# RWKV attention and a small mixture of experts on one core: weights in column blocks, the first input chunk on a second DMA queue, and the first key mixes built another way

## What is computed

```python
shifted = jnp.pad(hidden, ((0, 0), (1, 0), (0, 0)))[:, :-1]
key   = hidden * time_mix_key   + shifted * (1.0 - time_mix_key)
value = hidden * time_mix_value + shifted * (1.0 - time_mix_value)
rec   = hidden * time_mix_receptance + shifted * (1.0 - time_mix_receptance)
k, v, r = key @ Wk, value @ Wv, jax.nn.sigmoid(rec @ Wr)
rwkv = _wkv(time_decay, time_first, k, v)   # a scan over the tokens
x = _layernorm(x + (r * rwkv) @ Wo)
# then: router over 8 experts, top 2, silu, gated sum, residual, layer norm
```

## Time and profile before

| | us |
|---|---|
| median of three runs | 459.97 (459.67 to 460.25) |
| profiled execution, first to last instruction (span) | 458.2 |
| TensorE busy | 444.6 (97% of the span) |
| VectorE busy | 404.1 (88%) |
| ScalarE busy | 356.0 (78%) |
| GpSimd busy | 312.0 (68%) |

### The profile page before, as it was taken

One profiled execution on the slowest core, in us unless ns is written; L12 is line 12 of the kernel. 1 busy time (PEld: TensorE's weight loads), 2 busy tenths in 40 slices (PEclk: granted clock), 3 DMA queues, 4 the chain that ended last, 5 costly groups with the idle time before them and its releaser, 6 DMA issues.

```text
span 458.2 us, 6679 instructions
## 1 busy us (share of the span) xinstructions
PE 444.6 (97%) x1984; PEld 340.2 (74%) x1984; DVE 404.1 (88%) x616; ACT 356.0 (78%) x801; POOL 312.0 (68%) x300
## 2 busy tenths in 40 slices
PE   8999999999999999999999999999999999999993
PEld 3444567777888888888888888888888888888761
DVE  5989989899788989999898998989898996876976
ACT  1666757877888779888788888888798887768695
POOL 2355677588658998579858797569966694744334
PEclk9999999999999999999999999999999999999998
DMA  8703230033000042002320042100520022300016
GB/s 239 223 0 117 93 92 1 1 115 93 1 1 0 2 160 92 24 0 74 135 70 0 1 139 93 46 0 24 162 93 1 1 69 94 137 1 0 0 49 229
DMA packets 20244, 30.64 MB, mean 67 GB/s; under 512 B 2032, under 2 KB 7152, under 8 KB 20208
## 3 DMA queue, kind: packets, MB, share of 16 engines
q1 hardware_dynamic: 20208, 30.21, 20.3%
HBM read 21.82 MB, written 8.39 MB: 66 GB/s over the span
## 4 chain that ended last, share of the span: by engine, by line
PE 78%; DVE 5%; ACT 2%; POOL 2%; issue 1%; ACTq 0%; DVEq 0%
PE PH L449 5%; PE PV L330 5%; PE PV L336 5%; PE PV L331 5%; PE PR L336 5%; PE PR L330 5%; PE PK L330 5%; PE PR L331 5%; PE PK L336 5%; PE PK L331 5%; PE PP L359 4%; PE PP L360 4%; PE PP L364 4%; PE PT L431 3%; PE PP L379 2%
## 5 line engine op out<-in xcount | busy, mean ns | idle before, releaser
L592 ACT ACTIVATE PR<-PR 128x512 f32<-128x512 f32 x128 | 74.6, 583 | 29.8 <-PE PR L336 10.6
L1213 POOL TENSOR_TENSOR DQ<-DEN,EX 128x512 f32<-128x512 f32 x32 | 41.3, 1290 | 20.6 <-DVE DEN L871 20.6
L1219 POOL TENSOR_SCALAR NM<-SUM,RS 128x1 f32<-128x1 f32 x30 | 8.0, 267 | 62.1 <-ACT RS L592 62.1
L330 PE MATMUL PK<-KH,WKH 128*128 128x512 f32 x112 | 46.2, 413 | 0.6 <-DVE NUM L888 0.6
L925 DVE SCALAR_TENSOR_TENSOR KT<-D,VEC,XT 128x512 f32<-128x512 f32 x57 | 45.8, 851 | 0.0
L330 PE MATMUL PV<-VH,WVH 128*128 128x512 f32 x112 | 45.6, 407 | 0.0
L336 PE MATMUL PR<-RL,WRH 128*128 128x512 f32 x112 | 44.0, 393 | 0.7 <-POOL RL L1181 0.7
L330 PE MATMUL PR<-RH,WRH 128*128 128x512 f32 x112 | 44.5, 398 | 0.2 <-DVE RW L912 0.2
L336 PE MATMUL PV<-VL,WVH 128*128 128x512 f32 x112 | 43.9, 392 | 0.0
L336 PE MATMUL PK<-KL,WKH 128*128 128x512 f32 x112 | 43.9, 392 | 0.0
L331 PE MATMUL PK<-KH,WKL 128*128 128x512 f32 x112 | 43.8, 391 | 0.0
(11 more groups left out here) (275 smaller groups left out, 1285.7 us busy)
## 6 DMA issues: line engine op xcount, KB each, us to landing
XT<-in_xt SPq DMA_DIRECT2D x32, 256.0 KB, 3.3
XN<-in_x SPq DMA_DIRECT2D x28, 256.0 KB, 2.7
out<-XN SPq DMA_DIRECT2D x28, 256.0 KB, 2.0
X1T<-in_wo SPq DMA_DIRECT2D x1, 1024.0 KB, 5.1
XT<-in_x SPq DMA_DIRECT2D x4, 256.0 KB, 4.2
out<-XT SPq DMA_DIRECT2D x4, 256.0 KB, 2.4
X1T<-in_wk SPq DMA_DIRECT2D x2, 256.0 KB, 4.9
XN<-in_wv SPq DMA_DIRECT2D x2, 256.0 KB, 5.7
```

The source lines that it names most:

```text
L330: eng.matmul(dst[:, :], wh[:, c, o], high[:, c, :], start=(c == 0), stop=False)
L592: eng.activation(*a, **k).then_inc(q[s], 1)
L1213: eng.tensor_tensor(DQ[:, :], DEN[:, 0:T], EX[:, 1, :], ALU.add).then_inc(q["e"], 1)
```

## The change

Three things are changed together. (1) The host lays the three weight matrices out as `[partition, column block, 4 x 128]`, so that one column block is 2 KB without a gap in each partition; loads, products and low parts index them accordingly. `key(4)` now waits only for the first half of the low parts of wk. (2) Input chunk 0 is requested by ScalarE's queue before its table load; SP requests VEC, the first block of wk and then input chunks 1, 2, 3; the remaining blocks follow in another order (wk 1, wv 0, wr 0, wk 2-3, wv 1, wr 1, wv 2-3, wr 2-3). (3) The four key mixes of batch 0 no longer use D: ScalarE makes y = (1 - mix) * shifted into the mix's own tile, with OMK = 1 - mix computed by VectorE from VEC, and VectorE makes hidden * mix + y in place (`first_mix`). GpSimd makes all four differences of batch 0, and VectorE's `difference` goes. Beside these, the dummy products fall from four to two.

```diff
-            def load_w(dst, src, s, lo=0, hi=H):
-                eng.dma_start(dst[:, :, lo:hi], src.rearrange("(c p) n -> p c n", p=128)[:, :, lo:hi])\
-                   .then_inc(q[s], 16)
+            def load_blocks(which, i):
+                dst, src = ((X1T, wk), (XN[0], wv), (XN[1], wr))[which]
+                lo, hi = ((0, 1), (1, 2), (2, C))[i]
+                eng.dma_start(dst[:, lo:hi, :], src[:, lo:hi, :]).then_inc(q[f"ws{which}{i}"], 16)
 
             eng.dma_start(VEC[:, :, :], vec).then_inc(q["vec"], 16)
-            load_xt(0, 0)
+            load_blocks(0, 0)
             load_xt(0, 1)
-            load_w(X1T, wk, "ws00", 0, 128)
             load_xt(0, 2)
             load_xt(0, 3)
-            for i, (lo, hi) in enumerate(((0, 128), (128, 256), (256, H))):
-                if i:
-                    load_w(X1T, wk, f"ws0{i}", lo, hi)
-                load_w(XN[0], wv, f"ws1{i}", lo, hi)
-                load_w(XN[1], wr, f"ws2{i}", lo, hi)
+            for which, i in ((0, 1), (1, 0), (2, 0), (0, 2), (1, 1), (2, 1), (1, 2), (2, 2)):
+                load_blocks(which, i)
@@ tensor
-                    last = eng.matmul(dst[:, :], stage[:, c, o], full(0, which, c), start=(c == 0), stop=(c == C - 1))
+                    last = eng.matmul(dst[:, :], stage[:, u, 128 * c:128 * c + 128], full(0, which, c), start=(c == 0), stop=(c == C - 1))
...
-                    eng.wait_ge(q[("lwk", "lwv", "lwr")[which]], j + 1 if which else 2)
+                    eng.wait_ge(q[("lwk", "lwv", "lwr")[which]], j + 1 if which else j // 2 + 1)
...
-            for _ in range(4):
+            for _ in range(2):
                 eng.matmul(PP[:, :], RW[:, 0, 0:128], RW[:, 0, :], start=True, stop=True)
@@ scalar
+            eng.dma_start(XT[:, 0, 1:T + 1], xt[0, 0:128, :]).then_inc(q["xt0"], 16)
             eng.preload_act_table_set(TABLES)
...
             act("etd", NTD, VEC[:, 0, :], ACT.Exp)
+            eng.wait_ge(q["om"], 1)
+            eng.wait_ge(q["cm"], 1)
+            for c in range(C):
+                eng.wait_ge(q[f"xt{c}"], 16)
+                act("y", full(0, 0, c), XT[:, c, 0:T], ACT.Copy, scale=OMK[:, c:c + 1])
@@ vector
+            def first_mix(c):
+                eng.wait_ge(q[f"xt{c}"], 16)
+                eng.wait_ge(q["y"], c + 1)
+                eng.scalar_tensor_tensor(out=full(0, 0, c), in0=XT[:, c, 1:T + 1], scalar=VEC[:, 2, c:c + 1],
+                                         in1=full(0, 0, c), op0=ALU.mult, op1=ALU.add).then_inc(q["kt"], 1)
...
+            eng.wait_ge(q["vec"], 16)
+            eng.tensor_scalar(OMK, VEC[:, 2, :], -1.0, 1.0, ALU.mult, ALU.add).then_inc(q["om"], 1)
...
-            difference(1)
-            mixes(0, 0, 0, 1)
-            difference(3)
-            mixes(0, 0, 2, 3)
+            for c in range(C):
+                first_mix(c)
             mixes(0, 1, 0, 1)
@@ gpsimd
-            difference(0, 0)
-            difference(0, 2)
+            for c in range(C):
+                difference(0, c)
...
-                    o = slice(128 * j, 128 * j + 128)
-                    eng.tensor_tensor(low[:, :, o], stage[:, :, o], high[:, :, o].bitcast(F32), ALU.subtract)\
+                    eng.tensor_tensor(low[:, j, :], stage[:, j, :], high[:, j, :].bitcast(F32), ALU.subtract)\
@@ host
+    def blocks(w):
+        return np.ascontiguousarray(np.asarray(w).reshape(C, 128, C, 128).transpose(1, 2, 0, 3)).reshape(128, C, H)
```

More of the change, by code:

```diff
@@ L49, in rwkv_moe_postln @@
         VEC = sb("VEC", [128, 5, C])
-        CST = sb("CST", [128, 4, C])
+        CST = sb("CST", [128, 5, C])
         XT = sb("XT", [128, C, T + 1])
@@ L86, in rwkv_moe_postln @@
         UPT = KT[:, 1, :]
-        TD, NTD, CC, QB = (CST[:, i, :] for i in range(4))
+        TD, NTD, CC, QB, OMK = (CST[:, i, :] for i in range(5))
         def full(b, which, c):
@@ L251, in store, with load_rows @@
                 eng.dma_start(out[b, 128 * n:128 * n + 128, :], xn_at(NT * b + n)).then_inc(q[f"out{n}"], 16)
[L253 to L255 removed]
+            def load_rows(dst, src, s, n=H):
+                eng.dma_start(dst[:, :, 0:n], src.rearrange("(c p) n -> p c n", p=128)).then_inc(q[s], 16)
+            def load_blocks(which, i):
+                dst, src = ((X1T, wk), (XN[0], wv), (XN[1], wr))[which]
+                lo, hi = ((0, 1), (1, 2), (2, C))[i]
+                eng.dma_start(dst[:, lo:hi, :], src[:, lo:hi, :]).then_inc(q[f"ws{which}{i}"], 16)
             eng.dma_start(VEC[:, :, :], vec).then_inc(q["vec"], 16)
[L258 removed]
+            load_blocks(0, 0)
             load_xt(0, 1)
[L260 removed]
             load_xt(0, 2)
             load_xt(0, 3)
[L263 to L267 removed]
+            for which, i in ((0, 1), (1, 0), (2, 0), (0, 2), (1, 1), (2, 1), (1, 2), (2, 2)):
+                load_blocks(which, i)
             for c in range(C):
@@ L272, in _ @@
             eng.wait_ge(q["k"], C)
-            load_w(X1T, wo, "wo")
-            load_w(DR, dr, "dr", 0, HD)
+            load_rows(X1T, wo, "wo")
+            load_rows(DR, dr, "dr", HD)
             eng.wait_ge(q["lwv"], C)
@@ L310, in whole @@
             def whole(dst, stage, u, which):
-                o = slice(128 * u, 128 * u + 128)
                 eng.wait_ge(q[f"ws{which}{min(u, 2)}"], 16)
@@ L325, in split @@
                     eng.wait_ge(q["hw"], which + 1)
-                    eng.wait_ge(q[("lwk", "lwv", "lwr")[which]], j + 1 if which else 2)
+                    eng.wait_ge(q[("lwk", "lwv", "lwr")[which]], j + 1 if which else j // 2 + 1)
                 for c in range(C):
+                    o = slice(128 * c, 128 * c + 128)
                     if first:
                         eng.wait_ge(q["hi"], C * (3 * (b - 1) + which) + c + 1)
-                    eng.matmul(dst[:, :], wh[:, c, o], high[:, c, :], start=(c == 0), stop=False)
-                    eng.matmul(dst[:, :], wl[:, c, o], high[:, c, :], start=False, stop=False)
+                    eng.matmul(dst[:, :], wh[:, j, o], high[:, c, :], start=(c == 0), stop=False)
+                    eng.matmul(dst[:, :], wl[:, j, o], high[:, c, :], start=False, stop=False)
                     if first and C * (3 * (b - 1) + which) + c + 1 == ODD:
@@ L335, in split @@
                         eng.wait_ge(q["lo"], by_pool(C * (3 * (b - 1) + which) + c + 1))
-                    last = eng.matmul(dst[:, :], wh[:, c, o], low[:, c, :], start=False, stop=(c == C - 1))
+                    last = eng.matmul(dst[:, :], wh[:, j, o], low[:, c, :], start=False, stop=(c == C - 1))
                     if j == C - 1 and c < C - 1:
@@ L914, in mix @@
             def mix(b, which, c):
-                if b:
-                    eng.wait_ge(q["d"], C // 2 + C * (b - 1) + c + 1)
-                else:
-                    eng.wait_ge(q["d0" if c % 2 else "d"], c // 2 + 1)
+                eng.wait_ge(q["d"], C * b + c + 1)
                 if b and which < 2:
@@ L1038, in _ @@
             eng.tensor_scalar(QB, CC, -1.0, CLIP, ALU.mult, ALU.add).then_inc(q["cc"], 1)
-            def difference(c):
-                eng.wait_ge(q[f"xt{c}"], 16)
-                if c == 1:
-                    eng.wait_ge(q["cm"], 1)
-                eng.tensor_tensor(D[:, c, :], XT[:, c, 1:T + 1], XT[:, c, 0:T], ALU.subtract).then_inc(q["d0"], 1)
             def low_weights(lo):
@@ L1338 @@
         "vec": np.ascontiguousarray(np.stack(rows).transpose(2, 0, 1)),
-        "wk": np.ascontiguousarray(L0_attn_Wk),
-        "wv": np.ascontiguousarray(L0_attn_Wv),
-        "wr": np.ascontiguousarray(L0_attn_Wr),
+        "wk": blocks(L0_attn_Wk),
+        "wv": blocks(L0_attn_Wv),
+        "wr": blocks(L0_attn_Wr),
         "wo": np.ascontiguousarray(L0_attn_Wo),
```

1 line of the change is left out of this document (removed), and 2 rows, old and new, of the table q.

## The result

| | median us | ratio to before |
|---|---|---|
| before, beside it | 460.11 (459.67 to 460.95, 4 runs) | |
| after | 463.92 (463.82 to 464.44, 4 runs) | 1.0083 (95%: 1.007 to 1.0095) |

A forecast was written before the change was run, and what follows sets the result against it. The prediction took TensorE's pace to bound the kernel once started, so its time follows the start of `scan_max(0)`. Gains of 0.8 us (landing) and 0.7 us (shorter chain), all else nothing, gave 458.5 us, range 457.5 to 459.7.

The forecast's parts named there:

- So whatever moves the start earlier moves the whole: Start of the kernel: a shift there moves the whole 450 us behind it; the rest matters only if it slows the steady part.
- Layout and the wait of `key(4)`: nothing: Weight loads, low parts and the start of `key(4)`: claimed to cost or gain nothing.
- Chunk 3 lands at 7.0: Last input chunk at the start: lands at 7.0 and not 7.8, gain 0.8 us, bounds 0.4 and 1.7.
- rival B: Start: chunk 3 comes no sooner (7.8) or part is given back; only 0.7 us gained, 459.3 us; chance 0.18.
- From landing to `scan_max(0)`, 2.76 us: Start, chunk 3's landing to `scan_max(0)`: y, mix 3 and two value mixes take 2.76 us, 0.67 us gained.
- GpSimd's differences beside the mixes: Start: four GpSimd differences beside VectorE's mixes cost 0 to 0.42 us for each of three mixes; taken as 0.
- rival C: TensorE at the start: clock doesn't rise at about 5 us, `scan_max(0)` 0.65 us later, 460.6 or 463.6 us; chance 0.09.
- The second queue: Chunk 0 requested by ScalarE: the first issue comes 0.44 us sooner; by the skill's rule alone chunk 3 lands at 7.37.
- The signs of being wrong: Profile after: 0.85 us spacing in `key(0)`, y 3 starting after 7.5, or `value(1)`'s gain absent at 100 us.
- The sum: Whole kernel: span 458.2 less 1.5 gives 456.7 us; with 1.8 us around it, 458.5 us.

The follow-up runs named there:

- b_blocks: The kernel before with only the weights in column blocks, old request order on SP's one queue: 460.90 us, ratio 1.0015.
- b_cst5: The kernel before with only CST enlarged from four rows to five, the fifth unused: 462.76 us, ratio 1.0055.
- a_bm: The changed kernel with each weight column block as a separate contiguous 256 KB in memory: 463.21 us, ratio 1.0065.
- a12_xt1first: The changed kernel with CST of twelve rows, and SP requesting chunk 1 ahead of wk block 0: 462.82 us, ratio 1.0059.
- best1: The changed kernel with CST of 20 rows, padding before TH, chunk 1 before wk block 0, four dummies, GpSimd's differences 2 and 3 after six mixes: 459.24 us.
- a12_gate: The changed kernel with CST of twelve rows, and GpSimd making differences 1 to 3 only after the four key mixes: 463.83 us, ratio 1.0083.
- a12_oneq: The changed kernel with CST of twelve rows, and chunk 0 requested by SP, no DMA on ScalarE: 464.41 us, ratio 1.0093.

## Why the prediction was wrong, step by step

**"So whatever moves the start earlier moves the whole."** Right, with the other sign: 1.27 us at `scan_max(0)`, 1.26 at `value(1)` (23.15 for 21.89) and 1.23 at 100 us. The other half of that sentence, that the rest matters only if it slows the steady part, was right too, and was not followed up.

**"Layout and the wait of `key(4)`: nothing."** This is the step that failed most. The layout does cost nothing (b_blocks, spacing 229.6). But the change has another edit, one more row in CST, which the prediction only weighed as work for VectorE. It moved every tile behind it by 32 bytes and cost about 2.5 to 2.75 us (b_cst5 2.55). No term of the sum, no rival and no bound covered it. The one thing in the trace of before that hinted at it is that projections were spaced 234.2 ns and the others 229.6 although all are the same operation.

**"Chunk 3 lands at 7.0", bounds 6.07 and 7.37.** It landed at 8.07, outside the bounds and later than before. The first piece came 0.15 later than the model has it (3.41 for 0.72 + 1.6 + 0.94 = 3.26). The model, a constant time for each piece, failed: from chunk 0 to chunk 1 lie 3.3 us for two pieces, and then only 0.67 us for each. The later pieces are faster than any bound I took (0.75), the gap ahead of them was in no row I read. Its cause stays open. With contiguous blocks chunk 3 landed at 7.57 (a_bm), and with chunk 1 in second place at 7.26 (a12_xt1first), inside the bounds, but with the same requests at 7.97 in best1. The starting point was one trace too: four other traces with the loads of before have chunk 3 at 7.3 to 7.8, so that a step of 0.8 was hardly more than the spread of the thing it was measured from. The prediction put rival B's landing at 7.8 as the worst case.

**From landing to `scan_max(0)`, 2.76 us.** It took 4.50. ScalarE's y took 0.72 instead of 0.62 (0.10). Mix 3 could start at 8.86 then and started at 9.80 (0.94), because mix 2 still held VectorE: it had waited behind a difference and took 1.52. That the chunks came only 0.67 us apart is not the reason: in a12_gate they came as close, and mix 3 started 0.83 after its y did, as 8.95 would be here. So 0.09 of the 0.94 is the step from y to mix and 0.85 is GpSimd. Mix 3 held VectorE for 1.44 us and not 0.66 (0.78, GpSimd again). The value mixes were 0.08 shorter. 0.10 + 0.94 + 0.78 - 0.08 = 1.74, which is the difference; 1.63 of it is the turns that VectorE and GpSimd take.

**GpSimd's differences beside the mixes, "I take 0", bound 0.42 each.** This term of the sum was mis-sized, by reading the early rows from one side only. The mix beside the difference at 6.74 was this one of the kernel before:

```profile
6.29 0.74 DVE L925 SCALAR_TENSOR_TENSOR DR<-D,VEC,XT 128x512 f32<-128x512 f32 x1
```

It started first, ended at 7.03 and kept its 0.74; the difference started second, ended at 7.93, 0.90 after it, and paid with 1.19 for 1.03. Near 57 us the mix started second: GpSimd's instruction ends at 58.28 and the mix at 58.82, 0.54 behind it, which is why it takes 1.17. Both are the turns that a12_gate shows. So 0.42 was no bound: what a mix pays depends on how much of the difference is still to come, and after the change two mixes paid 0.77 each (1.52 for 0.75), as the difference beside them had only just got its turn.

**The clock, rival C.** Half right. Its condition was met: the dummies ended at 5.21, wk block 0 came at 5.96, and two pairs ran at 1.2 GHz. Its price of 0.65 us was not, as VectorE was so late that the slow pairs hid behind it: `scan_max(0)` does not wait for TensorE at all in the changed kernel, and 0.2 to 0.4 us in its variants.

**The second queue.** The forecast counted only the issue that it saves, and a12_oneq shows that. What it did not count is that VEC lands 0.8 us later beside it. That is hidden, because y 0 needs chunk 0 too (3.41), but VectorE's small operations on CST then lie beside GpSimd's first difference, and one of 128x4 takes 0.95 instead of 0.16 and ends with the difference.

The signs of being wrong that the prediction named all came: 0.85 us spacing in `key(0)`, y 3 after 7.5, and no gain at 100 us.

The sum put right: start 1.07 (landing) + 1.74 (mixes) = 2.8 us later than the forecast 9.76, that is 1.27 later than before; steady part + 2.7; together + 4.0 on the span of 458.2, or 462.2 and not 456.7.

## What to carry to other kernels

When a kernel's time is TensorE without gaps, write down the addresses of both operands of its matmuls before and after any edit that adds, enlarges or reorders a tile, and look at the spacing of starts per product: an unused row of 16 bytes moved this kernel by 0.55%. Before moving work to GpSimd, find rows in which it overlaps the VectorE instructions on the path, look at both durations, and ask which of the two started first; the price falls on the other. A landing time in a trace is one draw: the same requests put chunk 3 up to 0.5 us apart here. Look at a few traces before a forecast rests on a step of that size.
